# Spread the token ids in DRAM, halve the second norm around a split feed-forward piece, and reorder the first microseconds

## The reference, cut to what matters

```
# 1. a transformer block (16 heads of 16, FF = 1024), H = 256
out = layernorm(x, g1, b1) @ (sf_w * mask).T + sf_b ;   x1 = x + out
q, k, v = linear(layernorm(x1, g2, b2))
att = relu(q k^T / 4) * causal ;  att = att / (sum(att) + 1e-9)
x2 = x1 + (att v) @ wo.T + bo
y  = x2 + relu(layernorm(x2, g3, b3) @ ff1.T + b) @ ff2.T + b
x  = layernorm(x + y)                       # the kernel's "ln4"
# 2. a mixture of 8 experts, top 1
e = argmax(x @ centroids.T) ;  alpha = sigmoid(x . centroid_e)
h = relu(layernorm(x, g_e, b_e) @ w1_e.T + b1_e)
out = layernorm(x + alpha * (x + h @ w2_e.T + b2_e) + (1 - alpha) * x)
```

## Time and profile before

| | |
|---|---|
| Median of 3 runs | 940.46 us (940.33 to 940.73) |
| The profiled execution's own time, its span | 937.14 us, 935.4 us |
| Mean granted TensorE clock | 0.989 |
| Busy: PE, PEld, DVE, ACT, POOL | 95%, 65%, 50%, 33%, 31% |
| The chain that ended last: PE, DVE, POOL, issue | 78%, 10%, 3%, 3% |
| First to last batch's query matmuls | 23.9 to 535.9 us |
| The 39 slots | from some 605 us to the end |

### The profile page before, as it was taken

The page is one execution under the profiler, slowest core; times in us unless marked ns, Lnnn a source line. Parts: engine busy times, 40 slices in busy tenths (PEclk is TensorE's granted clock), DMA queues, the critical chain, the costliest instruction groups (busy, mean ns, idle before and its releaser), DMA issues.

```text
span 935.4 us, 15985 instructions
## 1 busy us (share of the span) xinstructions
PE 890.0 (95%) x5752; PEld 607.1 (65%) x5752; DVE 470.3 (50%) x1339; ACT 306.2 (33%) x579; POOL 294.3 (31%) x406
## 2 busy tenths in 40 slices
PE   8888999979998999999999999999999999999994
PEld 5425456546544645645655654658999999999993
DVE  5256346425533734644644743633675555555552
ACT  1332432421442342342253153331433333333330
POOL 3213111131141132124105106133464544544432
PEclk9999999999999999999999999999999999999997
DMA  6200200061043004003004013421678666665720
GB/s 227 74 2 0 69 1 1 24 23 46 1 40 52 1 24 68 1 24 69 0 25 110 4 46 61 145 80 42 192 134 282 199 187 210 202 197 187 222 85 0
DMA packets 33715, 78.47 MB, mean 84 GB/s; under 512 B 10435, under 2 KB 24004, under 8 KB 27366
## 3 DMA queue, kind: packets, MB, share of 16 engines
q1 hardware_dynamic: 28310, 67.36, 26.6%
q0 software_dynamic: 4896, 9.56, 3.8%
q10 hardware_dynamic: 432, 0.54, 0.2%
HBM read 68.68 MB, written 9.67 MB: 84 GB/s over the span
## 4 chain that ended last, share of the span: by engine, by line
PE 78%; DVE 10%; POOL 3%; issue 3%; ACT 2%; DMA 2%; another core or an unknown queue 1%; DVEq 0%; POOLq 0%; SPq 0%; ACTq 0%
PE ps L502 14%; PE ps L520 14%; PE ps L410 11%; PE ps L418 9%; PE ps L367 9%; PE ps L383 7%; PE ps L336 3%; PE ps L351 3%; PE ps L344 3%; PE ps L284 2%; DMA arena<-in_x 2%; DVE st_ln L613 2%; DVE xh L626 2%; DVE arena L715 1%; DVE arena L671 1%
## 5 line engine op out<-in xcount | busy, mean ns | idle before, releaser
L715 DVE SCALAR_TENSOR_TENSOR arena<-ps,arena 128x1024 f32<-128x1024 f32 (+1 forms) x80 | 80.9, 1011 | 193.0 <-PE ps L367 183.5
L1113 ACT ACTIVATE arena<-ps 128x1024 f32<-128x1024 f32 (+1 forms) x80 | 95.5, 1194 | 211.1 <-DVE arena L715 208.4
L520 PE MATMUL ps<-w_sb,arena 128*128 x624 | 147.3, 380 | 0.0
L418 PE MATMUL ps<-ff2T,hT 128*128 128x256 f32 x512 | 120.9, 386 | 0.8 <-ACT hT L1099 0.8
L520 PEld LDWEIGHTS ps<-w_sb,arena 128*128 128x128 f32 x624 | 113.1, 191 | 12.2 <-issue 0.2
L410 PE MATMUL ps<-xT,ff1T 128*128 128x512 f32 x256 | 119.4, 605 | 1.0 <-DVE xT L757 1.0
L418 PEld LDWEIGHTS ps<-ff2T,hT 128*128 128x128 f32 x512 | 94.7, 191 | 31.8 <-issue 19.1
L502 PEld LDWEIGHTS ps<-arena 128*128 128x128 f32 x928 | 108.1, 192 | 1.4
L367 PE MATMUL ps<-arena 32*128 32x384 f32 (+3 forms) x1024 | 93.3, 468 | 15.9 <-ACT arena L1113 14.2
L502 PE MATMUL ps<-arena 128*128 128x128 f32 x928 | 108.3, 275 | 0.0
L1240 POOL TENSOR_TENSOR rs_ln<-mv_ln,eps 128x4 f32<-128x4 f32 x32 | 6.7, 209 | 317.6 <-DVE mv_ln L620 317.6
(11 more groups left out here) (155 smaller groups left out, 1115.2 us busy)
## 6 DMA issues: line engine op xcount, KB each, us to landing
arena<-in_w SPq DMA_DIRECT2D x29, 1024.0 KB, 4.8
wts<-in_w SPq DMA_DIRECT2D x10, 1024.0 KB, 5.1
w_sb<-in_w SPq DMA_DIRECT2D x8, 1024.0 KB, 4.8
arena<-in_epack SPq DMA_DIRECT2D x39, 134.0 KB, 2.3
token_store<-x SPq DMA_DIRECT2D x8, 520.0 KB, 3.6
arena<-in_x SPq DMA_DIRECT2D x8, 512.0 KB
ff1T<-in_ff SPq DMA_DIRECT2D x1, 1024.0 KB, 8.5
ff2T<-in_ff SPq DMA_DIRECT2D x1, 1024.0 KB, 9.8
```

The source lines that it names most:

```text
L418: last = eng.matmul(quarter(6, t), hT[:, m, t * P:(t + 1) * P], ff2T[:, m, :], start=m == 0, stop=m == FM - 1)
L520: last = eng.matmul(ps[:, 4 + j % 2, 0:H], shT[u][:, f, :], w2_sb[:, bass.ds(at + f * H, H)], start=f == 0, stop=f == FM - 1)
L715: eng.scalar_tensor_tensor(out=o, in0=i, scalar=0.0, in1=m, op0=ALU.max, op1=ALU.mult).then_inc(s_sd, 1)
L1113: eng.activation(o, i, ACT.Relu).then_inc(s_sa, 1)
```

## The change

1. **Ids.** Each id takes 64 bytes in DRAM (`LANE = 16` words): table, scatter offsets, padding fill and id loads follow.
2. **Second norm.** Statistics, reciprocal root, normalising and transposes go by halves of two tiles. The piece L418 at the boundary is split: two of its matmuls (`m` 4, 5) run between output projection and transposes, two (6, 7) after the transposes. On DVE the feed-forward addition and ln4's aggregation move behind the third norm's; on POOL ln3 goes before ln4; on ACT the keys go before ln4, and in the last part the first slot's hidden layer goes before ln4.
3. **Start.** Three matmuls on zeroed data in place of six; the other constants are converted ahead of the wait for PE; DVE in place of POOL adds `x1` for batch 0. Waits that counted on the old places follow.

```diff
-    table = nc.dram_tensor("slot_table", ((NE + 1) * N_TOK, 1), I32, kind="Internal").ap()
+    table = nc.dram_tensor("slot_table", ((NE + 1) * N_TOK * LANE, 1), I32, kind="Internal").ap()
...
-            for _ in range(6):
+            for _ in range(3):
                 eng.matmul(ps[:, 7, :], warm[:, 0:P], warm, start=True, stop=True)
...
         def pe_ln2_T(eng, b):
-            eng.wait_ge(s_xh["ln2"], b + 1)
-            pe_transposes(eng, xh, (0, 1), s_T["ln2"])
+            for i in range(2):
+                eng.wait_ge(s_xh["ln2"], 2 * b + i + 1)
+                for kd in range(KD):
+                    for t in (2 * i, 2 * i + 1):
+                        last = eng.transpose(ps[:, kd, t * P:(t + 1) * P], xh[:, t, kd * P:(kd + 1) * P], ident)
+                    if i:
+                        last.then_inc(s_T["ln2"], 1)
...
+        def pe_ffn2_part(eng, b, t, part):
+            for m in part:
+                last = eng.matmul(quarter(6, t), hT[:, m, t * P:(t + 1) * P], ff2T[:, m, :], start=m == 0,
+                                  stop=m == FM - 1)
+            if t % 2 and FM - 1 in part:
+                last.then_inc(s_f2, 1)
...
             if more:
                 pe_sf(eng, b + 1)
-            pe_unit(eng, f, 2 * FM - 1)
+            else:
+                pe_ffn2(eng, f, NT - 1, 1)
             pe_proj_o(eng, b)
+            if more and b:
+                pe_ffn2_part(eng, f, NT - 1, (4, 5))
             if more:
                 pe_ln2_T(eng, b + 1)
+            if more and b:
+                pe_ffn2_part(eng, f, NT - 1, (6, 7))
...
         def dve_start(eng):
...
             last.then_inc(s_sfg, 1)
+            dve_first_constants(eng)
             eng.wait_ge(s_sfg, 2)
             eng.wait_ge(s_sfc, 1)
...
+            eng.wait_ge(s_const, 2)
+            eng.tensor_tensor(x1[:, :, :], xin[:, :, :], row(0), ALU.add).then_inc(s_pa0, 1)
...
         def dve_add_sf(eng, b):
...
-                last = dve_row_stats(eng, "ln2", x1, i)
-            return last
+                dve_row_stats(eng, "ln2", x1, i).then_inc(s_dve, 1)
+                eng.wait_ge(s_dve, dve.up())
+                for t in (2 * i, 2 * i + 1):
+                    last = eng.bn_aggr(mv["ln2"][:, t, :], stats["ln2"][:, t, :])
+                last.then_inc(s_var["ln2"], 1)
...
         def dve_ln2(eng, b):
...
-            dve_normalise(eng, b, "ln2", x1, xh)
+            for i in range(2):
+                eng.wait_ge(s_rs["ln2"], 2 * b + i + 1)
+                for t in (2 * i, 2 * i + 1):
+                    last = eng.tensor_scalar(xh[:, t, :], x1[:, t, :], mv["ln2"][:, t, 0:1], rstd["ln2"][:, t:t + 1],
+                                             ALU.subtract, ALU.mult)
+                last.then_inc(s_xh["ln2"], 1)
...
-            eng.tensor_copy(posi[:, :], pos1[:, :])
+            eng.tensor_scalar(posi[:, :], pos1[:, :], float(LANE), None, ALU.mult)
...
             if more:
-                dve_mean_var(eng, "ln2", dve_add_sf(eng, b + 1))
-            if b:
-                last = dve_add_ffn(eng, f, 1)
-            if more:
+                dve_add_sf(eng, b + 1)
                 dve_ln2(eng, b + 1)
                 dve_ln2_T(eng, b + 1)
-            if b:
-                dve_mean_var(eng, "ln4", last)
             dve_mean_var(eng, "ln3", dve_add_o(eng, b))
+            if b:
+                dve_mean_var(eng, "ln4", dve_add_ffn(eng, f, 1))
             dve_ln3(eng, b)
...
             act_queries(eng, b)
+            act_keys(eng, b)
             if g >= 0:
                 act_ln4(eng, g)
-            act_keys(eng, b)
...
+            slot_act_hidden(eng, 0)
             act_ln4(eng, f - 1)
-            slot_act_hidden(eng, 0)
...
+        def pool_rstd_ln2(eng, b):
+            for i in range(2):
+                v = rstd["ln2"][:, 2 * i:2 * i + 2]
+                eng.wait_ge(s_var["ln2"], 2 * b + i + 1)
+                eng.tensor_tensor(v, mv["ln2"][:, 2 * i:2 * i + 2, 1], eps4[:, 0:2], ALU.add).then_inc(s_eps["ln2"], 1)
+                eng.wait_ge(s_eps["ln2"], 2 * b + i + 1)
+                eng.tensor_tensor(v, v, nhalf[:, 0:2], ALU.pow).then_inc(s_rs["ln2"], 1)
...
+            pool_rstd(eng, b, "ln3")
             if b:
                 pool_rstd(eng, f, "ln4")
                 pool_shift4(eng, f)
-            pool_rstd(eng, b, "ln3")
...
             pool_rstd(eng, 0, "ln1")
-            pool_pre_a(eng, 0)
-            pool_rstd(eng, 0, "ln2")
-
-            eng.wait_ge(s_xh["ln2"], 1)
-            w = (NE + 1) * N_TOK // P // NT
+            pool_rstd_ln2(eng, 0)
+
+            eng.wait_ge(s_xh["ln2"], 2)
+            c, w = (NE + 1) * N_TOK // P, LANE // NT
             for t in range(NT):
-                eng.dma_start(table.rearrange("(p c) o -> p (c o)", p=P)[:, t * w:(t + 1) * w],
-                              padid[:, t * w:(t + 1) * w]).then_inc(s_scat[t], 16)
+                eng.dma_start(table.rearrange("(p c) o -> p (c o)", p=P)[:, t * w * c:(t + 1) * w * c].rearrange(
+                    "p (w c) -> p w c", w=w), padid[:, :].unsqueeze(1).broadcast_to([P, w, c])).then_inc(s_scat[t], 16)
...
-            eng.dma_start(ids[:, j:j + 1], table[bass.ds(at, P), :]).then_inc(d_ids[j % XN], 16)
+            eng.dma_start(ids[:, j:j + 1], table.rearrange("(r l) o -> r (l o)", l=LANE)[bass.ds(at, P), 0:1],
+                          allow_slow_non_contiguous=True).then_inc(d_ids[j % XN], 16)
```

More of the change, by code:

```diff
@@ L60 @@
 N_RING = KD * FF
+LANE = 16
 NORMS = ("ln1", "ln2", "ln3", "ln4")
@@ L184, in build @@
         s_x = sem("s_x")
-        s_warm, s_fill, s_const, s_sfg, s_sfc = (sem(f"s_{n}") for n in ("warm", "fill", "const", "sfg", "sfc"))
+        s_warm, s_fill, s_const, s_sfg, s_sfc, s_copied, s_pa0 = (
+            sem(f"s_{n}") for n in ("warm", "fill", "const", "sfg", "sfc", "copied", "pa0"))
         s_pa, s_pb, s_xb2, s_r2 = sem("s_pa"), sem("s_pb"), sem("s_xb2"), sem("s_r2")
@@ L416, in pe_ffn2 @@
                 eng.wait_ge(s_f1e, FM * b + FM)
[L417 to L421, removed]
+            pe_ffn2_part(eng, b, t, range(4 * half, 4 * half + 4))
         def pe_unit(eng, f, k):
@@ L633, in dve_ln1_stats, with dve_first_constants @@
             dve_mean_var(eng, "ln1", dve_row_stats(eng, "ln1", xin, 1))
+        def dve_first_constants(eng):
+            eng.wait_ge(s_fill, 1)
+            eng.wait_ge(s_load_c, 16)
+            eng.tensor_copy(triu_b[:, :], tri_u)
+            eng.tensor_copy(tri2.rearrange("p (c q) -> p c q", c=2), causal[:, 0:P].unsqueeze(1).broadcast_to([P, 2, P]))
+            eng.tensor_copy(tokf[:, :], tok0).then_inc(s_pos, 1)
+            for kd in range(KD):
+                eng.tensor_tensor(bkm[:, kd, :], col[:, C_ME:C_ME + 2], col[:, C_BK + kd:C_BK + kd + 1].broadcast_to([P, 2]),
+                                  ALU.mult)
+            eng.tensor_copy(base[:, :], ebase).then_inc(s_copied, 1)
         def dve_start(eng):
@@ L651, in dve_start @@
             eng.tensor_tensor(rowb[:, 0, :], ps[:, 1, 0:H], rowb[:, 0, :], ALU.add).then_inc(s_const, 1)
[L653 to L663, removed]
+            eng.wait_ge(s_const, 2)
+            eng.tensor_tensor(x1[:, :, :], xin[:, :, :], row(0), ALU.add).then_inc(s_pa0, 1)
         def dve_add_sf(eng, b):
-            eng.wait_ge(s_pa, b + 1)
+            eng.wait_ge(s_pa, b) if b else eng.wait_ge(s_pa0, 1)
             eng.wait_ge(s_rs["ln1"], b + 1)
@@ L1001, in dve_batch @@
             if more:
-                dve_mean_var(eng, "ln2", dve_add_sf(eng, b + 1))
-            if b:
-                last = dve_add_ffn(eng, f, 1)
-            if more:
+                dve_add_sf(eng, b + 1)
                 dve_ln2(eng, b + 1)
                 dve_ln2_T(eng, b + 1)
+            dve_mean_var(eng, "ln3", dve_add_o(eng, b))
             if b:
-                dve_mean_var(eng, "ln4", last)
-            dve_mean_var(eng, "ln3", dve_add_o(eng, b))
+                dve_mean_var(eng, "ln4", dve_add_ffn(eng, f, 1))
             dve_ln3(eng, b)
@@ L1014, in dve_program @@
             dve_start(eng)
-            dve_first_constants(eng)
-            dve_mean_var(eng, "ln2", dve_add_sf(eng, 0))
+            dve_add_sf(eng, 0)
             dve_ln2(eng, 0)
@@ L1073, in act_queries @@
             else:
-                eng.wait_ge(s_const, 3)
+                eng.wait_ge(s_copied, 1)
             for m in range(KD):
@@ L1251, in pool_pre_a @@
             eng.wait_ge(s_x, 16 * (b + 1))
-            if b:
-                eng.wait_ge(s_xh["ln2"], b)
-            else:
-                eng.wait_ge(s_const, 2)
+            eng.wait_ge(s_xh["ln2"], 2 * b)
             eng.tensor_tensor(x1[:, :, :], xin[:, :, :], row(0), ALU.add).then_inc(s_pa, 1)
@@ L1336, in pool_batch @@
                 pool_pre_a(eng, b + 1)
-                pool_rstd(eng, b + 1, "ln2")
+                pool_rstd_ln2(eng, b + 1)
             else:
@@ L1397, in sp_load_x @@
             if b:
-                eng.wait_ge(s_pa, b)
```

(1 more changed line is left out.)

## The result

Median 915.6 us (915.47 to 915.68, 5 runs), before 940.46 (939.59 to 942.48, 5 runs): ratio 0.9733, 95% interval 0.9719 to 0.9747. The profiled execution took 915.47 us, span 913.7: 21.67 less than before's, where the sum said 20.4.

The account below looks back on a forecast made before the run. TensorE (PE), 95% busy, was taken as the bound, with nameable waits. Terms -11.4 - 6.0 - 1.0 - 2.2 + 0.2 = -20.4 us took 937.14 to 916.7; plus 3.3 gave 920.0 us, range 914 to 928.

Parts of the forecast that it names:

- Part 1, the ids: Batches 2 and 3: ids 64 bytes apart end slow loads of x, DVE's two stops and the low clock, -11.4 us.
- many four-byte writes to a few neighbouring lines: Id scatters from batch 2 on: writes done one after another at the memory, engines' reads caught behind; behind the 11.40 us.
- rival C: Batches 2 and 3: the ids help by half, 5 us stay, 925 us; chance 0.10.
- Rivals A and B: Id scatters: A, spacing changes nothing, 931.5 us, chance 0.11; B, spacing makes writes slower, 966 us, chance 0.05.
- the unknown releaser of the 9.03 us: DVE's stop before an attention step at 208.00 us, read as an instruction fetch caught in the same queues.
- Part 2, -6.0: Boundaries 1 to 6: second norm by halves and split piece bring queries 1.0 us earlier each, -6.0 us.
- Rival D: Second norm: halves give nothing, each meeting a semaphore turn and POOL; 926 us, chance 0.07.
- Boundary 0, -1.0: Boundary without a feed-forward piece: only the norm's chain counts, -1.0 us (0.6 to 1.3).
- the start, -2.2: Kernel start: PE's constants 1.42 us earlier, a 0.99 us wait gone, less 0.2 for ACT's half: -2.2 us.
- The bound with early instructions staying slow: Kernel start: with fewer warming matmuls, early instructions stay at 0.85 us for longer, gain only -1.0 us.
- Part 4, +0.2: Last batch: ln4's numbers reach ACT later, delaying its copy for the feed-forward, +0.2 us (0 to +0.8).
- the runs' median lies 3.3 above it; kept: Whole kernel: the 3.3 us between median and profiled execution, unexplained by the profile, added to 916.7 for 920.0 us.

Follow-up runs that it names:

- e4: The changed kernel with ids 4 bytes apart and the experts' stretches 18 KB apart instead of 16: 918.33 us.
- e11: The changed kernel with ids 4 bytes apart and the experts' stretches 16.5 KB apart: 918.23 us.
- e2: The changed kernel with ids 4 bytes apart again and the table fill as in the changed kernel: 923.81 us.
- e8: The changed kernel with six warming matmuls on zeroed data at the start instead of three: 918.20 us.
- e5: The changed kernel again, unaltered, as yardstick on a second chip: 916.98 us.
- e1: The kernel before with only the ids spread to 64 bytes each: 926.45 us against 935.79, ratio 0.9903.
- e7: The changed kernel with the second norm as a whole, the feed-forward piece at the boundary still split: 926.38 us.

## Why the prediction came out as it did

The time was inside the range, the sum of the profiled execution 1.3 us too small, and the median 4.4 us too high.

**Part 1, the ids: right in place and size, wrong in its picture.** Batches 2 and 3 gave what was read from the rows, 6.93 + 4.46: 7.93 and 5.46 less the 1.0 each that any batch gained. What failed is the reading "many four-byte writes to a few neighbouring lines" (e4, e11). Against rival C it was no argument either: the number of ids per line was not the main matter, their common offset was. Rivals A and B fell. By the Trainium skill's rule that a transfer below 512 bytes does read-modify-write ("DMA: Bandwidth & Descriptors", Specifications) nothing should have changed. The ids are still four bytes, and their scatters land in 2.1 us where they took 5.2. The same page reports, under "Latency and other measured facts", that copies slow down at row pitches of large powers of two; its cases begin at 512 KB, and e4 and e11 show such an effect at 16 KB. It would have pointed to the lists' distance. That the unknown releaser of the 9.03 us was an instruction fetch was argued, and isn't shown. The stop went with the clog in the changed kernel, but e2 has the clog without it.

**Part 2, -6.0: right.** Batches 1 to 6 gained 1.21 + 5 x 1.0 = 6.2 (in batches 2 and 3, what is left besides the stall). Chain and PE do arrive together, as worked out: without the split the boundary loses 0.46 us (0.4 expected), without the halves 1.10 (1.0 expected). Neither alone gives what the two give. The cover of ln3's and ln4's later places held: no batch has a new wait ahead of its attention steps. Rival D fell.

**Boundary 0, -1.0, and the start, -2.2: right.** 0.93 and 2.35 measured. e8 shows that PE's order decides the start, at 1.2 of the 1.42 us that the step gave it. The bound with early instructions staying slow did not come up.

**Part 4, +0.2: right in place.** +0.37, ended by ACT's copy as expected.

**The step that failed by size: "the runs' median lies 3.3 above it; kept".** After the change the median lies 0.1 above the profiled execution. The offset was no property of a run outside its span. The kernel before varied from 934.00 to 942.48 us over four sets of runs, its two long batches lost 11.4 us in one profile, and with the same 4-byte spacing e2 lost 5.7 in another. e2's runs spread over 3 us, while those of the changed kernel spread over 0.2 (the result's) and 0.6 us (e5). It fits that the clog itself varied and the profiled execution had a mild case; no profile of a 940 us execution shows it, so this stays open. The other 1.2 us of the miss is POOL's last wait, which went with the table's layout in every profile; the prediction had no term for it.

## What to carry to other kernels

When small writes to DRAM go to several lists at once, try what distance the lists' starts have: with 4-byte ids and lists 16 KB apart, 512 bytes more between them did nearly what a table sixteen times as large did, and so did ids 16 bytes apart. Look for the cost not where the writes are issued but in the next transfers on the queues, by their time per packet. And when a norm stands between two matmul stages, split both: halves of the norm shorten the chain, a piece of other work cut in two fills PE's gaps, and each without the other gives half or nothing.

## What else the runs showed

**A low clock without a stop of its own.** In e1, e4 and e7 PE ran at the lower of its two levels, 1.2 GHz, for 3.4 us at the start of batch 1. Work ahead of it was the same in e4 and e5. Busy time by stage (length, PE, PEld, DVE, ACT, POOL, PEclk, DMA share, GB/s), first e4, then e5:

```profile
81.00:85.00 4.00, 4.00 (x7) 1.58 (x6) 2.78 (x10) 0.00 (x0) 0.96 (x2) 0.57 0.00 0
```

```profile
81.00:85.00 4.00, 4.00 (x10) 1.71 (x9) 2.88 (x10) 1.27 (x2) 0.85 (x2) 1.00 0.00 0
```

PE executes seven instructions in place of ten, and batch 1 lasts 73.07 us in place of 71.55. Both kernels had idled 0.16, 0.66 and 0.74 us at this boundary just before. Why one execution fell and the other didn't, the runs don't say. In e7 it accounts for 1.1 of the 1.7 us over my 7.7.

**The same kernel in two sets of runs.** The changed kernel took 915.60 us in the result's runs and 916.98 in e5's; the difference lies in the slots, in the waits with no known releaser shown above.
